# A decoder layer on one core: the empty-mask branch once for all batches, cross-attention with in-place exponentials and transposed value products

## What is computed

```python
# self-attention: 64 heads of 32, in 4 branches of 16 heads, T = 100
BRANCH_CONFIGS = [(16, 0), (128, 16), (128, 0), (256, 144)]
...
bmasks = jnp.stack([((dist >= g) & (dist < h)).astype(w.dtype) for h, g in BRANCH_CONFIGS], axis=0)
w = w * full_mask
probs = jax.nn.softmax(jnp.concatenate([w, sinks], axis=-1), axis=-1)
out = jnp.einsum('bhqk,bhkd->bhqd', probs[..., :T], v)
out = out + probs[..., T:] * v_nulls.reshape(1, H_TOT, 1, DH)
...
y = ctx @ WO + bO
return y.mean(axis=1)
```

```python
# cross-attention: 16 heads of 32, 722 keys, TOPK = 32
scores = jnp.einsum('bhqd,bhkd->bhqk', q, k) / SCALE
top_scores, top_idx = jax.lax.top_k(scores, eff_k)
w = jax.nn.softmax(top_scores, axis=-1)
top_v = jnp.take_along_axis(v[:, :, None, :, :], top_idx[..., None], axis=3)
out = jnp.einsum('bhqk,bhqkd->bhqd', w, top_v)
```

## Time and profile before

| | |
|---|---|
| median of 3 runs | 2792.08 us (2772.25 to 2794.88) |
| the profiled execution, its own time | 2798.57 us |
| its span | 2796.8 us |
| PE / PEld busy | 2325.4 / 1898.0 us |
| DVE / ACT / POOL busy | 2033.7 / 1411.8 / 1014.8 us |
| mean granted PE clock | 0.898 |
| self-attention, about 0 to 937 us | loop period 54.6 us |
| spectral block | about 937 to 978 us |
| cross-attention, about 978 to 2797 us | a batch every 105 to 112 us |

### The profile page before, as it was taken

The page is one execution under the profiler, slowest core; times in us unless marked ns, Lnnn a source line. Parts: engine busy times, 40 slices in busy tenths (PEclk is TensorE's granted clock), DMA queues, the critical chain, the costliest instruction groups (busy, mean ns, idle before and its releaser), DMA issues. The chain is left out here.

```text
span 2796.8 us, 47371 instructions
## 1 busy us (share of the span) xinstructions
PE 2325.4 (83%) x16760; PEld 1898.0 (68%) x16760; DVE 2033.7 (73%) x3866; ACT 1411.8 (50%) x3040; POOL 1014.8 (36%) x912
## 2 busy tenths in 40 slices
PE   3788788788878758899898898898899988988987
PEld 2556556555655447787787777777778877877875
DVE  4544544554454218899899899899898988998996
ACT  3222222122222125767667667667666666666663
POOL 3344335334533122343333343343333333333421
PEclk9898898889888779999999899999999999999987
DMA  4000000000000230000000000010000000000000
GB/s 157 7 19 9 9 18 9 9 9 18 9 9 12 79 97 14 25 15 14 25 19 15 15 28 15 15 28 14 15 26 17 15 16 28 15 15 23 14 1 7
DMA packets 37617, 63.03 MB, mean 23 GB/s; under 512 B 4014, under 2 KB 20542, under 8 KB 37420
## 3 DMA queue, kind: packets, MB, share of 16 engines
q1 hardware_dynamic: 35836, 56.28, 6.7%
q0 software_dynamic: 1584, 4.30, 0.5%
HBM read 53.99 MB, written 6.55 MB: 22 GB/s over the span
## 5 line engine op out<-in xcount | busy, mean ns | idle before, releaser
L1236 DVE MATCH_REPLACE8 ca_W<-ca_top,ca_W 128x722 f32<-128x722 f32 (+1 forms) x624 | 553.4, 894 | 0.0
L1227 DVE MAX8 ca_top<-ca_W 128x8 f32<-128x722 f32 (+1 forms) x624 | 536.3, 897 | 2.6
L883 POOL TENSOR_TENSOR ca_E<-ca_E,ca_S 128x722 f32<-128x722 f32 (+1 forms) x208 | 357.3, 1738 | 306.0 <-ACT ca_S L1088 305.9
L983 PE MATMUL ca_pO<-ca_V,ca_PT 128*128 128x64 f32 (+1 forms) x2496 | 347.1, 295 | 77.5 <-ACT ca_ctxT L1127 77.2
L983 PEld LDWEIGHTS ca_pO<-ca_V,ca_PT 128*128 128x128 f32 (+1 forms) x2496 | 334.8, 207 | 104.8 <-ACT ca_PT L1110 76.3
L865 POOL TENSOR_TENSOR ca_KL<-ca_K,ca_KH 128x384 fp32r<-128x384 f32 (+1 forms) x128 | 114.0, 891 | 508.9 <-ACT ca_KH L1081 508.9
L873 POOL TENSOR_TENSOR ca_cL<-ca_raw,ca_cH 128x768 fp32r<-128x768 f32 (+1 forms) x64 | 110.5, 1726 | 337.1 <-ACT ca_cH L1064 337.1
L1215 DVE MAX8 ca_top<-ca_S 128x8 f32<-128x722 f32 (+1 forms) x208 | 181.3, 901 | 58.0 <-ACT ca_S L1105 55.4
L88 PE MATMUL ca_pF<-ca_cH,ca_WkH 128*128 128x338 f32 (+1 forms) x512 | 194.3, 380 | 22.9 <-POOL ca_cL L873 22.9
L964 PE MATMUL ca_pT<-ca_ident,ca_E 128*128 128x128 f32 (+1 forms) x1248 | 190.4, 295 | 17.0 <-POOL ca_E L883 16.9
L1088 ACT ACTIVATE ca_S<-ca_W,ca_shift 128x722 f32<-128x722 f32 (+1 forms) x208 | 185.1, 890 | 38.6 <-DVE ca_W L1236 26.3
(11 more groups left out here) (204 smaller groups left out, 5256.4 us busy)
## 6 DMA issues: line engine op xcount, KB each, us to landing
ca_raw<-in_ctxT SPq DMA_DIRECT2D x32, 384.0 KB, 3.7
ca_raw<-in_ctxT SPq DMA_DIRECT2D x32, 338.0 KB, 3.0
sa_xin<-in_x SPq DMA_DIRECT2D x16, 200.0 KB
sa_xres<-in_x SPq DMA_DIRECT2D x16, 200.0 KB
x_scratch<-sa_x SPq DMA_DIRECT2D x16, 200.0 KB
ca_xin<-x_scratch SPq DMA_DIRECT2D x16, 200.0 KB
out<-ca_x SPq DMA_DIRECT2D x16, 200.0 KB
sa_E<-in_WQ SPq DMA_DIRECT2D x12, 256.0 KB, 13.2
```

Source lines behind the costliest of these rows:

```text
L883: pool.tensor_tensor(E[r][0:t.rows, :], E[r][0:t.rows, :], S[r][0:t.rows, :], ALU.subtract).then_inc(p_ready, 1)
L983: last = pe.matmul(out, PT[:, k, 0:t.rows], rhs, start=k == 0, stop=k == KC - 1)
L1227: n_of[t.i] = order.mark(dve.max(eight, w[rows, :]))
L1236: ins = dve.match_replace(w[rows, :], eight, (w if k else S[r])[rows, :], REMOVED)
```

## The change

**The fourth branch once.** `xsum` and `out3` get a column for each batch. The loop only sums the tokens; in the last body with `cur` PE multiplies all 16 sums at once (16 products of 16 columns), DVE finishes all `out3` in three steps, PE multiplies them with WO after the last y, DVE adds `bO`, and SP stores the 16 rows to HBM (`y_scratch`). In `cross_program` POOL begins with 16 DMAs that add row b of it to all 100 rows of x1 of batch b in HBM; the first `xin` load waits for all of them. L341, the wait for `out3_ready` ahead of the spreading and the addition L530 are gone.

**Cross-attention.** exp(S) is written over S and exp(W) over W; W has four buffers and E none; POOL subtracts W from S. `shift`, `1/Z` (now a power of -1) and QL and RL are made on POOL. `values` multiplies with V as the weights operand: for each key chunk and each of the tile's two heads a 32-row result with the queries as columns, at the head's place in pO, and 1/Z is spread by a product of the identity into the other half of pO. ACT copies both to NR once for a group of three tiles, POOL (for the rest tile DVE) multiplies them into ctxT. `output_T`, `normalise`, `late_tile` are gone. The lists of all engines are in a new order: q is projected in step 3 from a buffer qT of its own and split in step 5; x1's statistics move from step 4 to step 1, those of x2 from 2 to 3, the feed-forward product from 4 to 5 and the final sum from 4 to 6; PLAN is new; SP loads `xin` before the context.

```diff
-                if prev:
-                    pool.wait_ge(xres_in, b.count(16, 0))
-                    pool.tensor_tensor(xres[:, :], xres[:, :], bias_o[:, :], ALU.add).then_inc(xres_ready, 1)
...
-                    need(dve, v3_mm, b.count(1, 1))
-                    dve.tensor_reduce(xsum[:, :], xT[:, :, :], AX.X, ALU.add).then_inc(sum_ready, 1)
+                    at = bn.const if bn.reg is None else bn.reg + bn.const
+                    dve.tensor_reduce(xsum[:, :, bass.ds(at, 1)], xT[:, :, :], AX.X, ALU.add).then_inc(sum_ready, 1)
...
                     if br == 0 and prev:
                         pe.wait_ge(rden_ready, b.count(1, 0))
-                        pe.wait_ge(out3_ready, b.count(1, 0))
+                        if not cur:
+                            pe.wait_ge(out3_ready, 1)
...
-                if cur:
-                    pe.wait_ge(sum_ready, b.count(1, 1))
-                    need(pe, x1_ready, b.count(1, 0))
+                if cur and not nxt:
+                    pe.wait_ge(sum_ready, B)
+                    pe.wait_ge(x1_ready, b.count(1, 0))
...
-    PLAN = [([12, 13], []), ([], [0, 1]), ([2], [3]), ([4, 5], [6]), ([], [7, 8]), ([9], [10]), ([11], [])]
+    PLAN = [([12], [13]), ([], [0, 1]), ([2], [3, 4]), ([5], [6]), ([], [7, 8]), ([9], [10]), ([], [11])]
...
+            for i in range(B):
+                pool.dma_start(x1_dram[i], y3_dram[i:i + 1, :].broadcast_to((T, D)),
+                               accum_op=ALU.add).then_inc(x1_whole, 16)
...
+            def weights(tb, tp, t):
+                r, rows = ring(t, tp), slice(0, t.rows)
+                pool.wait_ge(e_ready, tb.count(NT, t.i + 1))
+                pool.wait_ge(f_ready, tb.count(NT, t.i + 1))
+                pool.tensor_tensor(S[r][rows, :], S[r][rows, :], W[r][rows, :], ALU.subtract).then_inc(p_ready, 1)
...
+                pool.wait_ge(z_ready, tb.count(NT, t.i + 1))
+                pool.tensor_tensor(rZ[rows, r:r + 1], Z[rows, r:r + 1], minus_one[rows, :], ALU.pow).then_inc(rz_ready, 1)
...
                 pe.wait_ge(pt_ready, tb.count(NT, t.i + 1))
-                need(pe, ot_ready, tb.count(NT, t.i))
+                pe.wait_ge(rz_ready, tb.count(NT, t.i + 1))
...
+                at = T * (t.g % 2)
+                for _, cols, to, g, q in t.blocks():
+                    pe.matmul(pO[to:to + DH, DEN + at + q.start:DEN + at + q.stop],
+                              rZ[:, r:r + 1].broadcast_to((128, DH)), ident[:, cols], start=True, stop=True)
                 for k in range(KC):
-                    last = pe.matmul(out, PT[:, k, 0:t.rows], rhs, start=k == 0, stop=k == KC - 1)
-                last.then_inc(o_mm, 1)
+                    for _, cols, to, g, q in t.blocks():
+                        last = pe.matmul(pO[to:to + DH, NUM + at + q.start:NUM + at + q.stop],
+                                         V[tp][:, k, 128 * g + to:128 * g + to + DH], PT[:, k, cols],
+                                         start=k == 0, stop=k == KC - 1)
+                        if k == KC - 1:
+                            last.then_inc(o_mm, 1)
```

471 lines of the change are left out of this document (258 added, 213 removed).

## The result

The changed kernel is slower: 2867.41 us (median of 4 runs, 2863.38 to 2868.18) against 2793.48 (4 runs); the ratio is 1.028, 95% interval 1.023 to 1.033. The forecast was 2552 us. The profiled execution took 2866.4 us where it took 2796.8 before.

The account below looks back on a forecast made before the run. It took PE with holes to bound self-attention, and DVE and PE together cross-attention. 2796.8 - 108 + 5 - 138 + 2.5 = 2558, less 6.5 for the profiled run's excess over the median: 2552 us; range 2478 to 2655.

Parts of the forecast that it names:

- Self-attention: Self-attention loop: removing the wait for out3 and the work around it saves 7.2 us a batch, -108 us over fifteen batches.
- Busy times of cross-attention: Cross-attention, per batch: PE busy 95.0 us at a clock of 0.93, 88.3 at full clock; POOL at 60 of 98.
- the prediction's first case: Cross-attention value products: two column groups run in parallel, the wider block sets the pass, 0.85 us a tile plus 0.15.
- serial loads: Rival, cross-attention value products: weight loads run in series, 27.2 us a batch instead of 16.0; 2720 us, chance 0.05.
- the 142 ns product: Rival, cross-attention: each small product costs 142 ns as in L624, 54.8 us for 386; 3021 us, chance 0.03.
- Exponentials in place cost nothing new: Cross-attention scores: overwriting S adds no cost, since its next copy follows right behind the transposing in ACT's order.
- Between transposing the weights and the product nothing lies any more: Cross-attention PE, most of seven steps: the copy L1110 and the inverse show, about 1.1 us a step, 7.7 a batch.
- DVE at 95.7 and PE between 96.0 and 102.7 feed each other: Cross-attention period: from these two engines' needs, 98.5 us a batch was taken; -138 us over fourteen batches.
- the 9.85 us: Cross-attention: forecast saving per batch, from 108.35 us to 98.5.
- q's head start of 7.5: Start of cross-attention: the first score no longer waits behind q, since q is made and split earlier; -7.5 us.
- Its own test: Signs of being wrong: L1082 at 75 ns or more, DVE over 5 us a batch for scores, PE waiting for hT.
- slower: Whole kernel: chance 0.06 of a slower outcome, with 0.03 for small products and 0.03 for accumulating DMAs delaying xin.

Follow-up runs that it names:

- e2: Changed kernel with S not in place (two E tiles, exp(W) into S, two W tiles), same orders on every engine: 2872.46 us.
- e18: e5 with S not in place, the old order of score copies and second scores, and accumulating DMAs behind the setup loads: 2696.47 us.
- e5: Changed kernel with the current tiles' exponentials moved from the end of ACT's step to ahead of the second transposed-weights copy: 2771.25 us.
- e19: e5 with the old table of projection slices and the accumulating DMAs behind the setup loads: 2730.66 us.
- e12: e1 with the accumulating DMAs issued only when cross-attention's setup and weight loads have landed: 2701.57 us.
- e1: Kernel before with only the self-attention part of the change, accumulating DMAs included: 2712.33 us.
- e15: e13 with the current tiles' exponentials back at the end of ACT's step: 2812.47 us.
- e13: e5 with exp(W) in its picks' step, subtraction behind POOL's low key parts and first context low part, x2 + bias_f earlier, rounding and DMAs later: 2831.15 us.
- e6: Changed kernel with y, q and f ahead of the first transposing on PE: 2863.64 us.

## Why the prediction was wrong

It was wrong in sign. Against its sum of 2558 the profiled 2866.4 is 308 more: 279 in the batches of cross-attention (+141 for -138), 20 at their start, 9 in self-attention.

- *Self-attention* was right. The period is 48.2 for 47.4, 94 us gained for 103. The spreading follows the V products without idle time, y still stands behind it, and PE waits at L649 as forecast. The timeline of PE, the same stretch as the earlier trace rows:

```profile
504.82 0.86 PE L571 MATMUL sa_pt<-sa_rden,sa_ident 32*32 32x100 f32 x32
...
543.21 4.01 PE L649 MATMUL sa_pq<-sa_E,sa_pick 101*32 101x100 f32 x96 [5.61 <-POOL sa_E L354]
```

- *Busy times of cross-attention* were right. PE has 96.4 us a batch at a clock of 0.89 (95.0 at 0.93 forecast), DVE 93.6, POOL 46% of its time where I said near 60. The small matmuls, in dispute there, at the higher clock level:

```profile
2126.16 0.93 PE L1082 MATMUL ca_pO<-ca_PT,ca_V 128*32 128x56 f32 x24
...
2137.19 1.07 PE L1082 MATMUL ca_pO<-ca_PT,ca_V 128*32 128x44 f32 x23
...
2140.98 1.27 PE L1082 MATMUL ca_pO<-ca_PT,ca_V 128*32 128x28 f32 x23
```

  The three rows are tiles cut into 72 and 56, 84 and 44, 100 and 28 columns. In the trace the starts of their products stand 31, 38 and 46 ns apart on average, 62, 76 and 92 ns a pair: every pair has 128 columns, and the time goes with the wider block, as the prediction's first case has it. Of the rivals, serial loads and the 142 ns product are both out.

- *The step that failed* is "Exponentials in place cost nothing new: S is freed when transposed, and the copy into it comes right behind in ACT's order". The tile's life was costed, not the order: what the runs point to as the cost is that the copy has to come behind the transposing. With S freed earlier, but the orders kept, nothing changed (e2); with the order that this allows, on top of the early exponentials, 75 us went (e18), 3.8 of them at the start, where the DMAs were later too. That the same order in place would not have brought them is argued, not shown.

- *A second step is missing.* "Between transposing the weights and the product nothing lies any more" was seen and costed at 7.7 us a batch; the place ahead of the transposing was not looked at. There the new table has no slice in steps 1, 4 and 6 (the old one none in 1 and 4), y, f and the late value products no longer stand ahead of it, and ACT's list ends with 1.7 us of exponentials. PE waits there 14.7 us a batch, before 0.0. The exponentials are worth 96 us (e5), the table 41 (e19). The 7.7 itself was on the high side: PE waits 5.0 us a batch at the products for PT and the inverse.

- *"DVE at 95.7 and PE between 96.0 and 102.7 feed each other"* took busy time plus the waits seen before, with the removed ones struck out. The removed waits were 8.1 on PE and 5.3 on DVE, and 7.7 and 1.7 were expected to be left; the engines are idle 21 and 24 us a batch. By the runs above much of this hangs on the order of ACT's, POOL's and PE's lists, which no sum over one engine shows. Even with the orders repaired (106.7 in e18) the period is not clearly below that of the old cross-attention (107.0 in e12), so no run found the 9.85 us that the transposed value products and the moved small work were to bring.

- *Start.* The accumulating DMAs were sized at +10 and cost 17.5 (e1); q's head start of 7.5 was not gained, and the new cross-attention starts 5 us later still. The score still waits for the low query parts, four in 4.5 us on POOL where DVE took 2.36:

```profile
977.54 4.51 POOL L942 TENSOR_TENSOR ca_QL<-ca_qT,ca_QH 32x400 fp32r<-32x400 f32 x4 [1.49 <-ACT ca_RH L1231]
```

- *Its own test* named the outcome, DVE waiting over 5 us a batch for scores, as a sign of being wrong; it waits 16.8. No rival had that as its mechanism, and "slower" was given 0.06.

Open: why the clock is higher in e15 than in e13, and what carries e18's 75 us: the first scores' copy, the second's with PE's own second scores, or S out of place; these were not separated. Whether the transposed products gain anything by themselves was not tried.

## What to carry to other kernels

When a change reorders several in-order engines, follow one turn of the ring from each engine's last wait to its first of the next step, and ask of every operation that moves what it covered in its old place, on both sides of the wait. Sharing a buffer in place may cost by the orders that it forbids, even where freeing it earlier in the same order brings nothing; cost those orders before sharing. That a consumer waits does not make it the bound: if its producer's next instruction starts microseconds after its input was there, look at that engine's own list first.

## What the runs showed of the hardware

- L1082, 32 weight columns on two column groups in turn, starts a product every 31, 38 or 46 ns on average at the higher clock level (45 tiles of each kind in the changed kernel, rows above), by whether the wider of its two blocks has 72, 84 or 100 columns. Behind a wait, at a granted clock of 0.50, it was 58 ns for the first kind (24 in 1.67 us from 2029.40 on). On four column groups in turn, 100 columns each, a product took 23 ns.
- Waits cost clock. After 4.2 us idle in e5 the transposes ran at a granted clock of 0.50 and the eight matmuls of y behind them at 0.62, in 5.77 us; with no such wait they take 3.60 at 1.00 (e6). The rows of e5:

```profile
1999.14 1.51 PE L1049 MATMUL ca_pT<-ca_ident,ca_S 128*128 128x128 f32 x6 [4.18 <-POOL ca_S L917]
2000.45 5.77 PE L1101 MATMUL ca_pX<-ca_WoT,ca_ctxT 128*100 128x512 f32 x8
```

- A DMA on POOL's queue that adds a row of one DRAM tensor to the 200 KB of another took 13.4 us from issue to landing (median of 16 issued together, beside the setup loads), where a plain load of 384 KB took 3.3:

```profile
x_scratch<-y_scratch POOLq DMA_DIRECT2D x16, 200.0 KB, 13.4
```

- POOL's subtraction of 32 x 400 elements took 1.1 us (four in 4.51), twice DVE's 0.57 and above the 0.96 that I had as its upper bound; a one-column power took 0.56 (mean in 1400 to 2600).
